# A two-layer block on one core: values become the loaded operand, and the heads' outputs come out turned

## What is computed

```python
q = (x @ wq.T + bq).reshape(Bx, Sx, H, DK).transpose(0, 2, 1, 3)
k = (x @ wk.T + bk).reshape(Bx, Sx, H, DK).transpose(0, 2, 1, 3)
v = (x @ wv.T + bv).reshape(Bx, Sx, H, DV).transpose(0, 2, 1, 3)
q, k = _rope(q, k)
scores = jnp.einsum('bhqd,bhkd->bhqk', q, k)
scores = jnp.where(causal[None, None], -jnp.inf, scores)
attn = jax.nn.softmax(scores / math.sqrt(DK), axis=-1)
out = jnp.einsum('bhqk,bhkd->bhqd', attn, v)
out = out.transpose(0, 2, 1, 3).reshape(Bx, Sx, H * DV)
return out @ wo.T + bo
```

## Time and profile before

| | |
|---|---|
| median of 3 runs (lowest, highest) | 2499.45 us (2493.75, 2513.72) |
| profiled execution, its span | 2502.42 us, 2500.5 us |
| PE busy | 2057.5 us, 82% of the span |
| DVE, ACT, POOL busy | 1680.5, 1187.7, 951.3 us |
| mean granted TensorE clock | 0.909 |
| L1065 (weighing), PE | 2560 instructions, 358.6 us |
| L1050 (turning), PE | 1280 instructions, 242.1 us, 116.3 us idle before them |
| L1542 (scan), DVE | 128 instructions, 374.8 us |

### The profile page before, as it was taken

How to read it: one execution, slowest core, us unless ns; L and a number is a source line. 1 busy time by engine, 2 the same in 40 slices (tenths; PEclk the granted TensorE clock), 3 DMA queues, 4 the chain that set the end, 5 groups by cost and what they waited for, 6 DMA issues and landing times.

```text
span 2500.5 us, 38952 instructions
## 1 busy us (share of the span) xinstructions
PE 2057.5 (82%) x11640; PEld 1430.8 (57%) x11640; DVE 1680.5 (67%) x2937; ACT 1187.7 (47%) x2702; POOL 951.3 (38%) x581
## 2 busy tenths in 40 slices
PE   4147788998899888998889878998889988989985
PEld 1013366665567556665566556665566655666764
DVE  2975678558965798558865788558876588645431
ACT  1214366345643466345653456344663456424631
POOL 0330366106920386106930277104850077203501
PEclk9558789999999999999999989998999998999997
DMA  2000002231123212231113212231123211142233
GB/s 103 0 0 17 17 35 71 91 109 43 57 70 113 69 51 74 90 110 40 61 64 119 68 42 84 67 106 56 43 68 116 85 45 55 65 133 71 71 105 116
DMA packets 82452, 175.06 MB, mean 70 GB/s; under 512 B 11448, under 2 KB 42560, under 8 KB 81984
## 3 DMA queue, kind: packets, MB, share of 16 engines
q1 hardware_dynamic: 78144, 164.05, 19.0%
q0 software_dynamic: 4096, 8.40, 1.1%
HBM read 123.71 MB, written 15.14 MB: 56 GB/s over the span
## 4 chain that ended last, share of the span: by engine, by line
PE 50%; DVE 22%; issue 14%; ACT 6%; POOL 4%; DMA 3%; SPq 1%; DVEq 0%; ACTq 0%; POOLq 0%
PE G L1065 7%; DVE HS L1542 7%; PE G L1050 5%; PE FM L1039 3%; PE FC L1027 3%; PE G L943 3%; PE G L954 3%; PE G L937 3%; ACT REG L1347 2%; DMA MW<-moe 2%; PE G L1082 2%; PE FM L907 2%; DVE maxes L1843 2%; DVE HC L1564 2%; PE FM L749 2%
## 5 line engine op out<-in xcount | busy, mean ns | idle before, releaser
L1542 DVE TENSOR_TENSOR_SCAN HS<-DA,D 128x1024 f32<-128x1024 f32 x128 | 374.8, 2928 | 20.5 <-ACT DA L1224 19.9
L1065 PEld LDWEIGHTS G<-REG 128*128 128x128 f32 x2560 | 350.4, 199 | 60.6 <-issue 50.2
L1065 PE MATMUL G<-REG 128*128 128x64 f32 x2560 | 358.6, 273 | 3.2 <-DVE REG L1855 3.2
L1967 POOL TENSOR_TENSOR Y<-Y,HC 128x1024 f32<-128x1024 f32 x114 | 269.1, 2361 | 181.3 <-DVE HC L1564 180.3
L1050 PE MATMUL G<-ident,REG 128*128 128x128 f32 x1280 | 242.1, 289 | 116.3 <-ACT REG L1347 114.0
L1347 ACT ACTIVATE REG<-G 128x128 f32<-128x128 f32 (+3 forms) x512 | 223.4, 436 | 121.4 <-PE G L1050 117.0
L1978 POOL TENSOR_TENSOR REG<-REG,cos_t 128x512 f32<-128x512 f32 x128 | 170.4, 1331 | 264.2 <-ACT REG L1323 264.1
L1050 PEld LDWEIGHTS G<-ident,REG 128*128 128x128 f32 x1280 | 149.0, 150 | 166.1 <-issue 132.6
L1339 ACT ACTIVATE REG<-G,maxes 128x128 f32<-128x128 f32 (+3 forms) x384 | 195.6, 510 | 81.9 <-DVE maxes L1843 81.9
L1981 POOL TENSOR_TENSOR REG<-REG 128x512 f32<-128x512 f32 x128 | 204.2, 1596 | 57.4 <-DMA REG<-ROT 48.8
L1039 PE MATMUL G<-REG 64*128 64x128 f32 (+3 forms) x768 | 217.8, 481 | 8.4 <-POOL REG L1981 7.4
(11 more groups left out here) (290 smaller groups left out, 4272.4 us busy)
## 6 DMA issues: line engine op xcount, KB each, us to landing
MW<-moe SPq DMA_DIRECT2D x120, 768.0 KB, 4.2
REG<-ROT SPq DMA_DIRECT2D x256, 128.0 KB
EW<-experts SPq DMA_DIRECT2D x16, 514.5 KB, 4.7
XG<-x_rows SPq DMA_DIRECT2D x8, 960.0 KB, 5.4
y_rows<-YO SPq DMA_DIRECT2D x120, 64.0 KB, 1.5
X<-xT SPq DMA_DIRECT2D x8, 256.0 KB, 6.1
W<-weights SPq DMA_DIRECT2D x1, 2048.0 KB, 9.5
REG<-xT SPq DMA_DIRECT2D x8, 256.0 KB, 3.2
```

Source lines behind the costliest of these rows:

```text
L1065: mm = pe.matmul(G[3][:, col:col + DK], PT[:, n % 2, c * P:(c + 1) * P], V[:, c, j * P + h * DK:j * P + (h + 1) * DK], start=c == 0, stop= ...
L1542: dve.tensor_tensor_scan(HS[:, :, :].rearrange("p h s -> p (h s)"), DA[:, n % 2, :, :].rearrange("p h s -> p (h s)"), D1[:, :, :].rearrang ...
L1967: pool.tensor_tensor(Y[:, :, :], Y[:, :, :], HC_EARLY if early else HC[:, n % 2, :, :], ALU.add).then_inc(y_add.sem, 1)
```

## The change

The weighing swaps its operands: 64 columns of V are loaded, and the turned probabilities are streamed, 128 columns a chunk. The output comes out turned, [64 head features, 128 queries], head 0 in partitions 0 to 63 of G3 and head 1 in 64 to 127. Both heads of a step are weighed in one call, behind the scores. ACT copies G3 to O when a pair is done. The inverses of the sums (DVE, `invert_sums`) lie on the query partitions; `spread_inverse` takes the place of `turn_out` and spreads each by a matmul with the identity over 64 rows. DVE multiplies O with that bank straight into the slot. The bias of the values is folded into bo once, in `late`. Apart from that, GpSimd's add of state n in `front` waits until the scan of state n+1 is over.

```diff
                 mm.then_inc(pt_mm.sem, 1)
-            def weigh_values(b, n):
-                j, i = n // PER_PAIR, n % PER_PAIR
-                h, t = tile_of(n)
-                pe.wait_ge(pt_copy.sem, pt_copy.at(b, n + 1))
-                if i == 0 and j:
-                    pe.wait_ge(o_d.sem, o_d.at(b, j))
-                elif i == 0:
+            def weigh_values(b, s):
+                j, t = s // TILES, s % TILES
+                pe.wait_ge(pt_copy.sem, pt_copy.at(b, 2 * s + 2))
+                if t == 0 and j:
+                    pe.wait_ge(o_copy.sem, o_copy.at(b, j))
+                elif t == 0:
                     pe.wait_ge(place_d.sem, place_d.at(b, 5))
-                col = t * P + h * DK
                 for c in range(t + 1):
-                    mm = pe.matmul(G[3][:, col:col + DK], PT[:, n % 2, c * P:(c + 1) * P],
-                                   V[:, c, j * P + h * DK:j * P + (h + 1) * DK], start=c == 0, stop=c == t)
-                mm.then_inc(pv_mm.sem, 1)
-            def turn_out(b, j):
-                pe.wait_ge(o_d.sem, o_d.at(b, j + 1))
+                    for h in range(2):
+                        mm = pe.matmul(G[3][h * DK:(h + 1) * DK, t * P:(t + 1) * P], V[:, c, j * P + h * DK:j * P + (h + 1) * DK],
+                                       PT[:, h, c * P:(c + 1) * P], start=c == 0, stop=c == t)
+                        if c == t:
+                            mm.then_inc(pv_mm.sem, 1)
+            def spread_inverse(b, j):
+                pe.wait_ge(rec_d.sem, rec_d.at(b, j + 1))
                 bank = take(b, ("out", j))
                 for t in range(TILES):
-                    mm = pe.transpose(bank[:, t * P:(t + 1) * P], O[:, t * P:(t + 1) * P], ident[:, :])
-                mm.then_inc(ot_mm.sem, 1)
+                    for h in range(2):
+                        mm = pe.matmul(bank[h * DK:(h + 1) * DK, t * P:(t + 1) * P],
+                                       rows[:, j % 2, 1, h * TILES + t:h * TILES + t + 1].to_broadcast([P, DK]), ident[:, :],
+                                       start=True, stop=True)
+                mm.then_inc(rinv_mm.sem, 1)
             def project_out(b, j):
                 if j == 0:
                     pe.wait_ge(p_exp.sem, p_exp.at(b))
-                pe.wait_ge(ot_copy.sem, ot_copy.at(b, j + 1))
+                pe.wait_ge(o_d.sem, o_d.at(b, j + 1))
                 pe.matmul(G[4][:, :], w("wo", j * D), ot_slot(j), start=j == 0, stop=j == PAIRS - 1,
...
                 pe.wait_ge(p_exp.sem, p_exp.at(b))
-                pe.wait_ge(ot_copy.sem, ot_copy.at(b))
+                pe.wait_ge(o_d.sem, o_d.at(b))
                 pe.wait_ge(gt_d.sem, gt_d.at(b))
...
                     turn(b, 2 * s)
-                    if s:
-                        weigh_values(b, 2 * s - 1)
                     if f is not None:
...
                     elif key[0] == "out":
-                        turn_out(b, key[1])
+                        spread_inverse(b, key[1])
                     elif key[0] == "turn":
                         turn_rows(b, key[1], take(b, key))
                     elif key[0] == "return":
                         returned = take(b, key)
                         if t is not None:
                             give_back(t, returned)
-                    if t_ == 0 and s + 2 < STEPS:
+                    if s + 2 < STEPS:
                         scores(b, s + 2)
-                    weigh_values(b, 2 * s)
-                    if t_ and s + 2 < STEPS:
-                        scores(b, s + 2)
-                weigh_values(b, N_TILES - 1)
+                    weigh_values(b, s)
+                spread_inverse(b, PAIRS - 1)
                 for j in range(PAIRS - 1):
                     project_out(b, j)
-                turn_out(b, PAIRS - 1)
             def front(b):
...
                 pe.wait_ge(s_late, n_late)
-                pe.wait_ge(s_made, 17)
+                for j in range(PAIRS):
+                    mm = pe.matmul(G[2][:, 0:1], w("wo", j * D), vec("bv", j), start=j == 0, stop=j == PAIRS - 1)
+                mm.then_inc(s_bv, 1)
+                pe.wait_ge(s_made, 18)
             def finish(t):
...
             def copy_out(b, j):
-                if j == 0:
-                    act.wait_ge(wo_mm.sem, wo_mm.at(b - 1))
-                    act.wait_ge(dn_mm.sem, dn_mm.at(b - 1))
-                    act.wait_ge(e2_mm.sem, e2_mm.at(b))
-                    act.wait_ge(yf_d.sem, yf_d.at(b))
-                act.wait_ge(ot_mm.sem, ot_mm.at(b, j + 1))
-                act.activation(ot_slot(j), ring_bank[("out", j)][:, :], ACT.Identity, bias=vec("bv", j)).then_inc(ot_copy.sem, 1)
+                if j:
+                    act.wait_ge(o_d.sem, o_d.at(b, j))
+                act.wait_ge(pv_mm.sem, pv_mm.at(b, PER_PAIR * (j + 1)))
+                act.activation(O, G[3][:, :], ACT.Copy).then_inc(o_copy.sem, 1)
             def early_scan(f, n, part, b):
...
                     copy_turned(b, 2 * s)
+                    if s and s % TILES == 0:
+                        copy_out(b, s // TILES - 1)
                     key = guest[s][0] if s in guest else (None, None)
...
                         add_bias(b, key[1])
-                    elif key[0] == "out":
-                        copy_out(b, key[1])
                     elif key[0] == "turn":
...
                                   negate=True).then_inc(nm_d.sem, 1)
-            def divide(b, j):
+            def invert_sums(b, j):
                 dve.wait_ge(p_exp.sem, p_exp.at(b, PER_PAIR * (j + 1)))
                 dve.reciprocal(rows[:, j % 2, 1, :], rows[:, j % 2, 0, :]).then_inc(rec_d.sem, 1)
-                if j:
-                    dve.wait_ge(ot_mm.sem, ot_mm.at(b, j))
-                dve.wait_ge(pv_mm.sem, pv_mm.at(b, PER_PAIR * (j + 1)))
-                dve.wait_ge(rec_d.sem, rec_d.at(b, j + 1))
-                dve.tensor_tensor(O.rearrange("p (t h d) -> p t h d", t=TILES, h=2),
-                                  G[3][:, :].rearrange("p (t h d) -> p t h d", t=TILES, h=2),
-                                  rows[:, j % 2, 1, :].rearrange("p (h t) -> p t h", h=2).unsqueeze(3).to_broadcast([P, TILES, 2, DK]),
-                                  ALU.mult).then_inc(o_d.sem, 1)
+            def divide(b, j):
+                if j == 0:
+                    dve.wait_ge(wo_mm.sem, wo_mm.at(b - 1))
+                    dve.wait_ge(dn_mm.sem, dn_mm.at(b - 1))
+                    dve.wait_ge(e2_mm.sem, e2_mm.at(b))
+                dve.wait_ge(o_copy.sem, o_copy.at(b, j + 1))
+                dve.wait_ge(rinv_mm.sem, rinv_mm.at(b, j + 1))
+                dve.tensor_tensor(ot_slot(j), O, ring_bank["out", j][:, :], ALU.mult).then_inc(o_d.sem, 1)
             def attention_end(b, following):
...
                         rotate(b, key[1])
+                    elif key[0] == "out":
+                        divide(b, key[1])
                     elif key[0] == "return" and t is not None:
                         give_back(t, ring_bank[key])
+                invert_sums(b, PAIRS - 1)
                 divide(b, PAIRS - 1)
...
                 dve.tensor_scalar(q_b, q_b, DK ** -0.5, None, ALU.mult).then_inc(s_made, 1)
-                dve.wait_ge(s_made, 17)
+                dve.wait_ge(s_bv, 1)
+                dve.tensor_tensor(vec("bo"), vec("bo"), G[2][:, 0:1], ALU.add).then_inc(s_made, 1)
+                dve.wait_ge(s_made, 18)
             def finish(t):
...
                 for n in range(STATES):
+                    if n + 1 < STATES:
+                        pool.wait_ge(scan_d.sem, scan_d.at(b, n + 2))
+                        pool.sem_inc(pool_passed, 1)
                     front_step(b, n)
```

13 lines of the change are left out of this document (7 added, 6 removed).

## The result

| | before | changed |
|---|---|---|
| median (lowest, highest), us | 2496.6 (2487.65, 2513.72), 4 runs | 2575.24 (2573.52, 2577.21), 4 runs |
| span of the profiled execution | 2500.5 us | 2572.0 us |
| mean granted TensorE clock | 0.909 | 0.899 |
| attention loops, in order | 138.1, 133.0 x3, 139.4 x3, 107.5 | 132.5, 144.3, 149.1 x5, 125.8 |
| start of the first attention loop | 298.3 us | 283.2 us |

The ratio is 1.0297, with a 95% interval of 1.0266 to 1.0328: slower. The forecast was 2540 in 2455 to 2610. The direction was right and the time in the range, 35 us above the point. The profiled executions differ by 71.5 us: the front gives 15.1 back, the eight loops take 85.6 more (1148.3 us in sum for 1062.7), and all that lies between them and behind them 1.0 more.

What follows compares the result with a forecast made beforehand. TensorE's own chain was taken to end each attention step, with DVE late in some. Seven loops +45.5, last loop +11.9, loop ends -1.6, `late` +1.5 and front -15 gave +42 us: 2540 us, range 2455 to 2610.

Steps and rivals of the forecast that it cites:

- The step on TensorE: TensorE's chain per attention step, last batch: 2.42, 4.2, 3.95 and 4.70 us for t = 0 to 3.
- entry and exit: TensorE entering and leaving column halves around the weighing: 0.10 + 0.05 us in, 0.10 + 0.06 us out.
- the spread as the guest: Spread of inverses in the t = 1 step: 0.86 us plus entry 0.26, where transposes took 0.45; step +0.85 us.
- Rivals B: Weighing and spread: the column halves don't run side by side, every pass takes 0.107 us alone; 2680 us, chance 0.17.
- rival C: Weighing and spread: entering column halves is free, 0.31 us a step and 0.2 a spread go; 2488 us, chance 0.17.
- The last loop: Attention loop of the last batch, no scan beside it: 11.9 us longer over its 32 steps, to 119 us.
- The other loops: Other seven attention loops: about half the steps run at PE's pace, so +6.5 us each, 45 in all.
- The clock: TensorE's granted clock in the attention loops: +19 or -19 us, taken as widening the range, not put into the sum.
- Rival D: Attention loops with a scan: earlier scores let DVE start sooner, -6 us in each of seven; 2455 us, chance 0.12.
- GpSimd's front: First front: with GpSimd's add waiting for the next scan, 15 scans of 3.47 us get shorter; -15 us.
- The end of the loop and `late`: Behind the loops turn_out and its copy go, -1.6 us; `late` adds 16 short matmuls, +1.5 us.
- my own case: Whole kernel: the forecast of 2540 us, widened by the clock to 2515 to 2580; chance 0.54.

Runs made afterwards that it cites:

- run 9: Changed kernel with the weighing at full width of 128 columns and half the matmuls, head 0's product left out, no column halves: 2494.37 us, ratio 0.9984.
- run 5: Changed kernel plus four transposes of the identity, which compute nothing, between the two turns for t = 1 to 3: 2512.92 us, ratio 1.0056.
- run 6: Changed kernel plus four transposes of the identity behind the weighing for t = 0 to 2, gap between the turns left open: 2553.04 us, ratio 1.0231.
- run 1: Kernel before with one edit alone, GpSimd's add in the first front waiting for the next state's scan: 2483.5 us, ratio 0.9938.
- run 3: Changed kernel with its weighing moved back between the turns, four buffers for turned copies, copy_out one place later: 2463.04 us, ratio 0.9859.
- runs 1 to 4: Before with front wait, 2483.5 us; before with new order, 2566.39; changed with weighing between turns, 2463.04; that with spread there too, 2478.79. Transposes were added to each.

## Why the prediction was right, and where it was short

*The step on TensorE: right.* The medians of the last batch are 4.23, 3.97 and 4.73 us for t = 1 to 3, where 4.2, 3.95 and 4.70 had been worked out; the steps with t = 0 take 2.4 to 3.4 us, where 2.42 had been. All the terms behind it hold: pairs 0.109 apart (0.107), the round trip 1.43 at t = 3 (1.39), entry and exit as for row halves, the spread as the guest that makes t = 1 the dearest. Rivals B and C fall with it. What rival C would have been worth is shown, but for the spread, by run 9: 2494 us where 2488 had been worked out (its parts add up to 2491). That they are so near is in part luck, as the clock, which C's sum left out, has a share in run 9.

*The last loop: mechanism right, size short.* It took 125.8 us, 122.6 at full clock, against 107.5 + 11.9 = 119.4 forecast. Of the excess of 6.4 us, 3.2 are the clock. Of the rest, 1.7 are in the eight steps with t = 0, which took 2.5 us more in sum than before, where 0.8 was forecast, and 1.0 in those with t = 2, which took 3.4 more, where 2.4 was. The last of these took 0.8 more by itself. I had let scores and mask cover the copy of the second tile, and at the end of the loop there are none:

```profile
2468.13 0.88 PE L1067 MATMUL G<-REG 128*64 128x128 f32 x12 [0.58 <-ACT REG L1352]
```


*The other loops: chain too dear.* At full clock the six middle ones grew by 4.9 us each and the first by 2.3, not by 6.5: 32 us in all where 45.5 were forecast.

*The clock: the step that failed.* I weighed it as a widening of plus or minus 19 us and set it to nothing in the sum, although I wrote that PE would idle more. It is a term of the sum, and has a sign: about 38 us. The gap's own idle is only part of what sets it. The longest waits in the gap come where ACT's copy is late in a loop with a scan. One of them, timelines of PE and of the other two engines in the fifth loop, and the window right behind the wait:

```profile
1470.54 0.66 PE L1051 MATMUL G<-ident,REG 128*128 128x128 f32 x2 [3.01 <-ACT REG L1352]
1470.99 1.92 PE L1028 MATMUL FC<-XN,W 128*128 128x512 f32 x2
...
1466.44 2.32 DVE L1544 TENSOR_TENSOR_SCAN HS<-DA,D 128x1024 f32<-128x1024 f32 x1 [0.56 <-ACT DA L1229]
1468.68 0.72 DVE L1839 SCALAR_TENSOR_TENSOR ROT<-FC,V_,sin_t 128x512 f32<-128x512 f32 x1
...
1469.43 0.69 ACT L1328 ACTIVATE REG<-FC,V_ 128x512 f32<-128x512 f32 x1 [2.57 <-DVE ROT L1839]
1470.02 0.38 ACT L1352 ACTIVATE REG<-G 128x256 f32<-128x256 f32 x1
```

```profile
1469.30:1476.10 6.80, 5.56 (x18) 2.19 (x18) 5.29 (x10) 3.16 (x8) 3.81 (x3) 0.50 0.21 77
```

A piece of the scan holds DVE for 2.32 us, its rotation comes late, ACT's `add_bias` (L1328) waits 2.57 us for that, and the copy (L1352) that the second turn needs stands behind it in ACT's queue. In the course of TensorE's wait of 3.01 us the clock fell to 1.2 GHz, and the same projection took 1.92 us instead of 1.02. With this term the sum is 47 - 15 + 1 + 38 = 71. That it closes proves nothing, as the 47 were got by taking the 38 off; what shows that the clock carries an amount of this size is run 5. The Trainium skill, "TensorE: Matmul & The Clock Gate", A second HAM failure mode, says that short idles of TensorE between groups of matmuls, where they come often, make the clock go up and down; the gaps of 0.56 and 0.78 us in every step and the clock of 0.89 agree with it, and run 6 adds that other work can make up for gaps that stay.

*Rival D: no.* DVE did not gain from scores that stand earlier. Waits in a middle loop, to be held against the earlier trace rows:

```profile
PE G L1051 <- ACT REG L1352: 22.6, 28, 3.0
...
DVE ROT L1839 <- PE FC L1028: 7.5, 5, 2.6
...
DVE maxes L1845 <- PE FM L1043: 5.1, 7, 1.4
```

Both of DVE's waits grew (3.7 to 7.5, 4.2 to 5.1), as TensorE's longer steps bring scores and projections later. In batch two of the changed kernel the wait for scores on FM did fall, to 2.6, but that on G rose from 0.4 to 3.8.

*GpSimd's front: right.* 15.1 us in the changed kernel, 14 of the median in run 1. *The end of the loop and `late`: right*, 1.0 us where about zero was forecast.

*The time: in part by the width of the range.* The chain was forecast 10 us too dear in sum (57 for 47), the clock 38 too cheap. 2575 lies 5 us inside the upper end of my own case (2515 to 2580), and the range of 155 us had been drawn around three cases of four, so that the time falling into it says little; the rows of a step and run 5 say more.

**What stays open.** What pattern of TensorE's work decides the clock. It is not the share of busy time over a loop: TensorE was busy 79% of the fourth loop of run 9 at 0.95, 84% of the fifth of run 3 at 0.93, 81% of the changed kernel's at 0.89 and 83% of that of before at 0.91. Nor is it settled why the transposes do so little for the whole time of runs 1 to 4, nor how far 0.47 us holds outside the two kernels that it was read from.

## What to carry to other kernels

An operation that stands between a producer and its round trip may be nearly free there; before making it cheaper by moving it, find what will stand in its place. Here the better form in the old place gave 2463 us and in the new place 2575, both with the front's 15 us gained. And where TensorE waits more, price the clock as a term of the sum with its sign, from two stretches of the same work at different clocks, and not as noise around it.
